# An MoE kernel's expert loop: ten tiles to a round, two of them half tiles, with each next tile's x transposed in the middle of a tile

## What is computed

```python
xn = _layernorm(x, axis=-1)                                  # x: (8, 2048, 256)
x = x + _L0_attn_ref(xn, W_qkv) + _L0_ffn_ref(xn, gate_w, ...)
# attention: one head of 256, causal, scores / 16
# ffn, on 16384 rows: shared swiglu 256 -> 512 -> 256, and
topk_ids = jnp.argmax(logits, axis=-1)                       # E = 32
xs = x * jax.nn.sigmoid(topk_val)[:, None]
sorted_x = xs[jnp.argsort(topk_ids)]
g = _grouped_mm(sorted_x, routed_gate_w, tokens_per_expert)
u = _grouped_mm(sorted_x, routed_up_w, tokens_per_expert)
d = _grouped_mm(jax.nn.silu(g) * u, routed_down_w, tokens_per_expert)
```

## Time and profile before

| | |
|---|---|
| median of 3 runs | 2384.75 us |
| profiled execution | 2384.18 us, its span 2382.2 us |
| mean granted TensorE clock | 0.992 |
| busy share of the span | PE 97%, PEld 90%, DVE 66%, ACT 51%, POOL 45% |
| token stage, expert stage, attention stage | about 0 to 703 us, 715 to 1445, 1451 to 2382 |
| instructions | 48635 |

### The profile page before, as it was taken

One profiled execution on the slowest core, in us unless ns is written; L12 is line 12 of the kernel. 1 busy time (PEld: TensorE's weight loads), 2 busy tenths in 40 slices (PEclk: granted clock), 3 DMA queues, 4 the chain that ended last, 5 costly groups with the idle time before them and its releaser, 6 DMA issues. The chain is left out here.

```text
span 2382.2 us, 48635 instructions
## 1 busy us (share of the span) xinstructions
PE 2316.4 (97%) x16118; PEld 2136.5 (90%) x16118; DVE 1565.0 (66%) x3322; ACT 1216.2 (51%) x2254; POOL 1065.6 (45%) x1031
## 2 busy tenths in 40 slices
PE   7999999999978999999999997999999999999998
PEld 6888888888868999999999995898988888888888
DVE  6777777777757777777777774646455555555555
ACT  3344434444425556656655653555555555555545
POOL 2333332333323333333333330666666666666667
PEclk9999999999998999999999999999999999999999
DMA  6665566665556766776767776334343444434331
GB/s 221 217 213 200 205 219 226 213 209 204 203 190 218 239 231 235 243 235 229 243 233 230 243 239 233 103 100 134 117 138 119 132 127 128 139 120 161 123 114 51
DMA packets 301977, 439.23 MB, mean 184 GB/s; under 512 B 35968, under 2 KB 209792, under 8 KB 301824
## 3 DMA queue, kind: packets, MB, share of 16 engines
q1 hardware_dynamic: 283712, 398.90, 48.9%
q0 software_dynamic: 18112, 38.37, 6.0%
HBM read 288.21 MB, written 148.96 MB: 184 GB/s over the span
## 5 line engine op out<-in xcount | busy, mean ns | idle before, releaser
L1231 POOL TENSOR_TENSOR t_p_lo<-t_score,t_p_hi 128x512 fp32r<-128x512 f32 (+1 forms) x320 | 360.0, 1131 | 190.7 <-ACT t_score L1355 113.9
L884 POOL DMA_INDIRECT ahead_rows<-xs_rows,ahead_slot x160 | 182.7, 1142 | 417.8 <-DMA ahead_slot<-token_of 257.7
L1347 ACT COPY t_score<-t_psS 128x512 f32<-128x512 f32 (+1 forms) x320 | 167.5, 523 | 332.5 <-PE t_psS L71 229.7
L1428 PE MATMUL t_psO<-t_v_hi,t_p_hi 128*128 128x258 f32 x1088 | 318.3, 293 | 0.9 <-DVE t_outb L1309 0.9
L1430 PE MATMUL t_psO<-t_v_hi,t_p_lo 128*128 128x258 f32 x1088 | 307.6, 283 | 0.0
L1432 PE MATMUL t_psO<-t_v_lo,t_p_hi 128*128 128x256 f32 x1088 | 306.6, 282 | 0.0
L1285 DVE TENSOR_TENSOR t_top<-t_top,t_psS 128x512 f32<-128x512 f32 (+3 forms) x264 | 155.1, 587 | 167.6 <-ACT t_score L1347 163.0
L305 POOL DMA_INDIRECT token_of<-a_token_i,a_slot_i x128 | 141.6, 1107 | 242.9 <-DVE a_slot_i L415 213.7
L69 PE MATMUL t_psS<-t_q_hi,ahead_x_hi 128*128 128x512 f32 (+3 forms) x640 | 233.8, 365 | 6.5 <-DVE t_q_lo L1267 5.5
L71 PE MATMUL t_psS<-t_q_lo,ahead_x_hi 128*128 128x512 f32 (+3 forms) x640 | 233.6, 365 | 0.0
L70 PE MATMUL t_psS<-t_q_hi,ahead_x_lo 128*128 128x512 f32 (+3 forms) x640 | 232.9, 364 | 0.0
(11 more groups left out here) (187 smaller groups left out, 7334.9 us busy)
## 6 DMA issues: line engine op xcount, KB each, us to landing
ahead_raw<-in_L_ffn_routed_gate_w SPq DMA_DIRECT2D x42, 512.0 KB
ahead_raw<-in_L_ffn_routed_up_w SPq DMA_DIRECT2D x42, 512.0 KB
ahead_raw<-in_L_ffn_routed_down_w SPq DMA_DIRECT2D x41, 512.0 KB, 5.0
e_raw<-in_L_ffn_routed_gate_w SPq DMA_DIRECT2D x41, 512.0 KB
e_raw<-in_L_ffn_routed_up_w SPq DMA_DIRECT2D x41, 512.0 KB
e_raw<-in_L_ffn_routed_down_w SPq DMA_DIRECT2D x41, 512.0 KB, 4.8
routed_rows<-e_dout SPq DMA_DIRECT2D x80, 256.0 KB, 4.4
a_xt<-in_L_attn_x SPq DMA_DIRECT2D x32, 512.0 KB, 5.9
```

The lines of the kernel that those rows point to most:

```text
L884: g.indirect_dma_start(out=xg[:, k, h], out_offset=None, in_=xs, in_offset=bass.IndirectOffsetOnAxis(slot[:, k, h:h + 1], 0)).then_inc(x_i ...
L1231: g_.tensor_tensor(p_lo[:, t % LR, c0:], score[:, t % SR, c0:], p_hi[:, t % HR, c0:].bitcast(F32), ALU.subtract).then_inc(lo_ok, 1)
L1347: s.copy(score[:, t % SR, c0:], psS[:, n % BANKS, c0:]).then_inc(u_act, 1)
L1428: nc.tensor.matmul(psO[:, a, 0:W], p_hi[:, kp, cols], v_hi[:, kv, j % J], start=j == 0, stop=False, skip_group_check=True)
```

## The change

- The expert loop runs in rounds of SETS = 10 tiles, of which places 4 and 9 hold half tiles of 128 rows; the first round is written out, the others are a loop of up to nine. An expert with c rows gets (c + 127) // 256 whole tiles, and a half tile where 1 to 128 rows are left. Whole tiles go to the eight whole places; half tiles to the half places, and to whole places if they don't fit.
- In a half tile x is stationary and the weights move, 512 columns at a time; h comes out with rows in partitions and is transposed (`h_transposes`) before `down_half`, which is done in the next step.
- `transposes(t + 1)` moves between the two halves q of `up(t)`, in a half tile between its gate and its up product; `x_high` and `x_low` move ahead with it.
- An expert's output rows lie together. Each tile's first row comes from a new table, `tile_row`, which SP reads before each store. The places behind are filled with zeros in 34 blocks of 128 rows instead of 32 of 256.
- `places()` makes constants on VectorE in the fifth group of the token stage; `tile_tables` is longer (30 operations instead of 16), and one more table row is copied.
- `keep.position` is made in the first round of the expert stage, two VectorE operations in each whole tile, and one at the end. In the attention stage its making goes; POOL waits there for the last stores before it gathers.

```diff
+SETS = 10
+HALVES = (4, 9)
...
+def is_half(j):
+    return j % SETS in HALVES
+
+
+def turns(j, i):
+
+    return SETS // 2 * i + j // 2
+
+
+def rows_moved(j, i):
+
+    k = j % 2
+    each = sum(1 if is_half(n) else 2 for n in range(k, SETS, 2))
+    return each * (i + j // SETS) + sum(1 if is_half(n) else 2 for n in range(k, j % SETS + 1, 2))
...
+            def places():
+
+                one, two = place_of[:, 0:1], place_of[:, 1:2]
+                then(v.tensor_scalar(by_ten[:], expert_f[:], float(SETS), None, ALU.mult))
+                then(v.tensor_scalar(tens[:], by_ten[:], float(SETS), token0[:, 0:1], ALU.add, ALU.is_le))
+                then(v.tensor_reduce(one, tens[:], AX.X, ALU.add))
...
             def tile_tables():
                 dve.wait_ge(seen_ok, J * NG + 1)
                 count = seen[:, NG % 2, 0]
-                then(v.tensor_scalar(tiles_i[:], count, float(ST - 1), None, ALU.add))
...
-                then(v.tensor_scalar(shift[:], shift[:], float(ST), None, ALU.mult))
+                full, whole = tiles_cum[:, 0, E - 1:E], tiles_cum[:, 1, E - 1:E]
+                index = wanted[:, 1:2]
+                flat = [a[:].rearrange("p a e -> p (a e)") for a in (tiles_cum, zeros, tiles, before_it, past, chosen, first_of)]
+                f_cum, f_zeros, f_tiles, f_before, f_past, f_chosen, f_first = flat
+                f_own, f_row = (a.rearrange("p a e -> p (a e)") for a in (own, row_of))
+                then(v.tensor_scalar(count_i[:], count, float(ST // 2 - 1), None, ALU.add))
...
+                v.tensor_scalar(tiles_i[:, 0], count_i[:], ST.bit_length() - 1, None, ALU.arith_shift_right)
+                then(v.tensor_scalar(tiles_i[:, 1], count_i[:], ST.bit_length() - 2, 1, ALU.arith_shift_right, ALU.bitwise_and))
...
+                then(v.tensor_scalar(more[:], by_eight[:, 0:SETS], full, None, ALU.is_lt))
...
+                then(v.tensor_reduce(rounds[:], more[:], AX.X, ALU.add))
...
+                if i == 4:
+                    places()
...
-            R = eng.value_load(keep.last_pair[0:1, 0:1], min_val=1, max_val=ET // 2 - 1)
-            for i in range(2):
-                for k in range(2):
-                    body(2 * i + k, k, i)
-            with eng.Fori(2, ET // 2) as i:
+            R = eng.value_load(keep.last_round[0:1, 0:1], min_val=1, max_val=ET // SETS - 1)
+            for j in range(SETS):
+                body(j, j, 0)
+            with eng.Fori(1, ET // SETS) as i:
                 with eng.If(i < R + 1):
-                    for k in range(2):
-                        body(2 * i + k, k, i)
+                    for j in range(SETS):
+                        body(SETS * i + j, j, i)
             return R
...
-            def load_slots(t, k, i):
-                wait_apart(sp, x_in[k], 16 * H * i, passed)
-                first = sp.value_load(keep.tile_slots[0:1, bass.ds(t, 1)], min_val=0, max_val=NS - 1)
-                sp.dma_start(slot[:, k], token_t[first]).then_inc(slot_in[k], 16)
-
-            def store(t, k):
-                wait(sp, do_ok, t + 1)
-                sp.dma_start(d_t[t], dout[:, k]).then_inc(d_out[k], 16)
+            def load_slots(t, j, i):
+                k = j % 2
+                wait_apart(sp, x_in[k], 16 * rows_moved(j - 2, i), passed)
+                unit = sp.value_load(keep.tile_slots[0:1, bass.ds(t, 1)], min_val=0, max_val=NS - 1)
+                if is_half(j):
+                    sp.dma_start(slot[:, k, 0:1], token_h[unit]).then_inc(slot_in[k], 16)
+                else:
+                    sp.dma_start(slot[:, k], token_t[unit]).then_inc(slot_in[k], 16)
+
+            def store(t, j):
+                k = j % 2
+                wait_apart(sp, do_ok, t + 1, passed)
+                row = sp.value_load(keep.tile_row[0:1, bass.ds(t, 1)], min_val=0, max_val=d_rows.shape[0] - ST)
+                if is_half(j):
+                    sp.dma_start(d_rows[bass.ds(row, P)], dout[:, k, 0]).then_inc(d_out[k], 16)
+                else:
+                    sp.dma_start(d_rows[bass.ds(row, ST)].rearrange("(p h) d -> p h d", h=H), dout[:, k]).then_inc(d_out[k], 16)
...
-            def step(t, k, i):
-                load_slots(t + 2, k, i + 1)
+            def step(t, j, i):
+                k = j % 2
+                load_slots(t + 2, j + 2, i)
                 load_up(t + 3, 1 - k)
                 load_down(t + 2, k)
                 if not is_first(t):
-                    store(t - 1, 1 - k)
+                    store(t - 1, j + SETS - 1)
...
+            def mul_half(t):
+                wait(dve, u_mm, Q * (t + 1))
+                wait(dve, silu_ok, Q * (t + 1))
+                wait(dve, hlo_ok, Q * t)
+                v.tensor_tensor(h32[:, 0], silu[:, 0], psU[:, 0].rearrange("p a n -> p (a n)"), ALU.mult).then_inc(h_ok, Q)
+
+            def h_low_half(t, k):
+                wait(dve, hhi_ok, Q * (t + 1))
+                v.tensor_tensor(h_lo[k][:, 0], psH[:], h_hi[k][:, 0].bitcast(F32), ALU.subtract).then_inc(hlo_ok, Q)
...
+            def positions(m):
+                ts = slice(m * TP, (m + 1) * TP)
+                wait(dve, pos_step, 2 * m)
+                v.tensor_tensor(moved[:], keep.one_hot[:, ts], keep.shift[:].unsqueeze(1).to_broadcast([P, TP, E]),
+                                ALU.mult).then_inc(pos_step, 1)
+                wait(dve, pos_step, 2 * m + 1)
+                v.tensor_reduce(begin[:, ts], moved[:], AX.X, ALU.add).then_inc(pos_step, 1)
...
+            def step(t, j, i):
+                k = j % 2
                 low(t + 1, 1 - k, 0)
-                mul(t, 0)
-                low(t + 1, 1 - k, 1)
-                h_low(t, k, 0)
-                mul(t, 1)
-                low_down(t, k)
-                x_low(t + 1, 1 - k)
-                h_low(t, k, 1)
-            tiles(dve, step)
+                if is_half(j + SETS - 1) and not is_first(t):
+                    h_low_half(t - 1, 1 - k)
+                if is_half(j):
+                    x_low(t + 1, j + 1)
+                    mul_half(t)
+                    low(t + 1, 1 - k, 1)
+                    low_down(t, k)
+                else:
+                    mul(t, 0)
+                    x_low(t + 1, j + 1)
+                    low(t + 1, 1 - k, 1)
+                    h_low(t, k, 0)
+                    mul(t, 1)
+                    low_down(t, k)
+                    if is_first(i):
+                        positions(sum(not is_half(n) for n in range(j)))
+                    h_low(t, k, 1)
...
+            def h_high_half(t, j, i):
+                wait(act, ht_mm, len(HALVES) * (i + j // SETS) + HALVES.index(j % SETS) + 1)
+                s.copy(h_hi[j % 2][:, 0], psH[:]).then_inc(hhi_ok, Q)
...
+                if is_half(j + SETS - 1) and not is_first(t):
+                    h_high_half(t - 1, j + SETS - 1, i - 1)
+                if is_half(j):
+                    silu_half(t)
+                    x_high(t + 1, j + 1)
+                    high(t + 1, j + 1, i, 1)
+                else:
+                    silu_of(t, 0)
+                    x_high(t + 1, j + 1)
+                    high(t + 1, j + 1, i, 1)
+                    h_high(t, k, 0)
+                    silu_of(t, 1)
+                    h_high(t, k, 1)
...
+            def up_half(t, j, i):
+                k = j % 2
+                wait(pe, xl_ok, t + 1)
+                for n, (psum, freed, out) in enumerate(((psG, silu_ok, g_mm), (psU, h_ok, u_mm))):
+                    wait(pe, wlo_ok, 2 * t + n + 1)
+                    wait(pe, freed, Q * t)
+                    for c in range(C):
+                        mm = split_matmuls(nc, psum[:, 0].rearrange("p a n -> p (a n)"), x_hi[:, k, c, 0:P], x_lo[:, k, c, 0:P],
+                                           part(whi, k, n)[:, c], part(wlo, k, n)[:, c], c == 0, c == C - 1)
+                    mm.then_inc(out, Q)
+                    if n == 0:
+                        transposes(t + 1, j + 1, i)
+
+            def h_transposes(t):
+                wait(pe, h_ok, Q * (t + 1))
+                for it in range(IT):
+                    mm = nc.tensor.transpose(psH[:, it * P:(it + 1) * P], h32[:, 0, it * P:(it + 1) * P], keep.ident[:])
+                mm.then_inc(ht_mm, 1)
...
+            def up(t, j, i):
+                k = j % 2
                 wait(pe, xl_ok, t + 1)
                 for q in range(Q):
+                    if q == 1:
+                        transposes(t + 1, j + 1, i)
...
-                up(t, k)
-                transposes(t + 1, 1 - k, i + k)
+            def step(t, j, i):
+                k = j % 2
+                if is_half(j):
+                    up_half(t, j, i)
+                else:
+                    up(t, j, i)
                 if not is_first(t):
-                    down(t - 1, 1 - k)
+                    if is_half(j + SETS - 1):
+                        down_half(t - 1, 1 - k)
+                    else:
+                        down(t - 1, 1 - k)
```

(31 more changed lines are left out.)

295 lines of the change are left out of this document (173 added, 122 removed).

## The result

The changed kernel takes **2552.08 us** (median of 4 runs, 2545.69 to 2555.02); the kernel before, beside it, 2385.36 (4 runs, 2382.60 to 2387.49). The ratio is 1.0696, 95% interval 1.0672 to 1.072: slower by 167 us. The forecast was 2424, with 2478 as its upper end. The direction was right; the size was missed by a factor of four.

What follows compares the result with a forecast made beforehand. TensorE, busy 97% of the span, was taken as the bound. Eight rounds at L = 13.4, half tiles' saving included, gave +34 us, clock +8, the rest -2: +40 on 2384.18, that is 2424 us; range 2345 to 2478.

Steps and rivals of the forecast that it cites:

- Half tiles, 64 us: Expert stage: a half tile takes TensorE 4.89 us instead of 8.87, 3.98 saved, times 16.
- Who waits for whom: Expert stage: TensorE's transposes of x wait for gathered rows, 80 to 110 us in all, longest near half tiles.
- the transposes of x wait for the gather in most tiles: Sign that the forecast is right: 80 to 110 us of such idle, whole steps of 9.5 to 10 us.
- 5 L + 26.0: Time in us of a round of ten tiles as five links; L is step start to x landed; at least 80.7.
- L = 13.4: Step start to x(t+2) landed after the change: 13.1 us, +0.7 table read, -0.4 loop turn; gives +34 us.
- Bounds 12.0 to 14.5: Lower and upper limits in us given for L, step start to x landed, around 13.1.
- Part *D: Rival: weight loads bind, half tiles needing 1.5 MB in 4.89 us; +10 us at most, counted in the range, no separate chance.
- Rival C: Weight and slot loads on SP slide with late x and share the gather's queue: L = 14.5, 2480 us; chance 0.15.
- Row table +0.7: In x's chain, the store on SP first reads its row number from a table: +0.70 us per link.
- Loop turn -0.4: In x's chain on SP, the loop's turn, 0.98 us, comes once in ten tiles instead of two: -0.4 on average.
- Clock +8: Expert stage: TensorE's clock falls after some waits, costing 8 us, between 0 and 25.
- The rest, -2: Tables +3, constants +1, skipped passes -3, positions -2, last half tile -1: sum -2 us, between -6 and +5.

Runs made afterwards that it cites:

- run 3: The changed kernel with slot numbers loaded one tile earlier, into five buffers in place of two: 2331.4 us, ratio 0.9787 to the kernel before.
- run 2: The kernel before with only the next x's transposes and split moved mid-tile, whole tiles only: 2551.65 us, ratio 1.0709.
- run 7: The whole-tile kernel with the mid-tile move, weight loads behind the first few cut to an eighth of their bytes: 2387.38 us, ratio 1.0009.
- run 8: The whole-tile kernel with the mid-tile move, down weights' load issued behind the next step's slot load: 2477.35 us, ratio 1.0396.
- run 1: The changed kernel with the next x's transposes and split back behind the second up half, half tiles kept: 2390.75 us, ratio 1.0031.
- run 6: The changed kernel with the store's row worked out from the round's number instead of read from the table: 2539.83 us, ratio 1.0644.
- run 5: The changed kernel with its eight rounds of ten tiles written out instead of a loop: 2538.49 us, ratio 1.0653.
- Run 12: The changed kernel with early slot numbers, and one gather in five held until its step has ended: 2441.63 us, ratio 1.0241.

## Why the prediction was wrong in size

**Half tiles, 64 us: right.** 62 in run 3. TensorE's steps were as worked out (a half step without a wait 6.06, with `down` of a whole tile in it).

**Who waits for whom: right.** Rows, in the two places near half tiles, and almost nothing on weights or VectorE. (Late before the change were three cases, not four: the wait of the earlier trace rows is one of the three of the earlier trace rows. No term of the sum hangs on it.) But only two waits per five tiles, not in most of them, and longer: "the transposes of x wait for the gather in most tiles" failed. In the steps between, 8.89 each, x was in time. The sum went by five equal links a round, 5 L + 26.0; in truth five tiles hang on one link that ends in the half step, one that starts behind it, and a plain step. With L = 13.4 for all of them that is 46.4 us instead of the 46.5 forecast, so this cost nothing; what cost was L.

**L = 13.4: the step that failed.** I took one L from the earlier trace rows, from a kernel in which x was in time and every tile whole, and kept it for every link. Bounds 12.0 to 14.5 held for one binding link only: the medians in the changed kernel are 14.5 where the half step asks, and 16.8 behind the half step; in run 2, without any half tile, the mean is 15.5. The two links' excess over 13.4, 1.1 and 3.4 us, is 4.5 us per five tiles, 72 us in all. The runs show three things that lengthen a link.

*The move.* `x_low` now stands ahead of the low part of the weights on VectorE, and SP's loads of the next weights, released by those, go out later: measured from the next step's start, the up weights at -1.3 us instead of -2.6 and the down weights at +0.5 instead of -0.2 (means of run 7, where x is almost never late, against the kernel before). The prediction had this slide at 1.3 us, and priced it at nothing, by the weights' two tiles of lead. The lead does cover the weights; it does not cover what stands behind them: store, slot load and gather queue with 0.5 to 1.5 MB. Run 8 takes away the order and gets 3.1 back (15.5 to 12.4), run 7 takes away the bytes and gets 5 (to 10.5).

*Lateness.* In run 2 the chain takes 15.9 us in the 54 steps in which TensorE waited, and 13.9 in the 15 in which it didn't. With the order of run 8 it is the other way round, 11.4 in the 34 with a wait and 13.5 in the 35 without. So lateness as such doesn't set the price; the order of the loads beside it does.

*The half step.* The link that starts behind it takes 16.3 us already in run 1, with the transposes late. So most of its excess is not the move's. The turn of the loop is part of it: 18.1 us with a turn, 16.0 without (17.9 and 15.5 in run 1). For the rest the trace shows only this: in run 1 the down weights go out 0.6 us behind the step start there, right ahead of the store, and before the step start in all other steps. That they are the cause is not shown; no run takes the half step's weights away by themselves. Part *D* had priced these loads at 10 us at most, again by their lead.

Rival C had the mechanism of the move, gave it 0.15 and L = 14.5, and its 2480 was still 72 us too low.

**Row table +0.7: right as a duration** (0.6 in run 6), but no link got shorter by it. **Loop turn -0.4: wrong in sign where it counts.** It comes once in ten, but one turn of the long loop costs SP 4 to 5.5 us instead of 1, in a chain that binds: about +14 (run 5). It takes the read of the row table to make it so long: in run 6 the turn costs 1.1. The two terms were priced apart, and their cost is in their meeting.

**Clock +8: wrong, about +64.** The stage is 895.4 - 670.8 = 224.6 us longer than in run 3, which does the same work; 164.2 - 4.0 = 160 are waits, and the other 64.4, 1.9 for each of 34 waits, are matmuls at the lower clock. The traces' clock records say the same: over the time in which TensorE was busy in the stage, what the granted clock fell short of full speed sums to 68.5 us in the change and 4.4 in run 3. Run 12 gives 2.0 a pause when nothing else is late. I had one row of a pause of 2.21 us and took 1 us a round; each round held four waits. Run 2 has 170.3 - 126.1 = 44 us in 60 waits of 2.1 us, 0.7 each. Set against the waiting, the clock adds 0.40 in the change, 0.35 in run 2, 0.38 in run 12.

**The rest, -2: +7 before the stage and +1.5 behind it.** Tables took 3 us more, as said, and TensorE waits 2.6 us for them in two places; TensorE's pause behind the loop's end went from 4.3 to 2.6, less than the 3 us promised, and the one at the entrance of the attention stage from 7.1 to 11.5, though that one lies between 6.5 and 12.6 in the other runs whatever their edit.

Together, on the stage: 64 predicted off, 62 came off; waits against a full TensorE 98 forecast, 160 came; clock 8 forecast, 64 came. 118 of the 128 us missed are in these two, and both grow from the one wrong assumption, that every link of the new kernel is as long as those of the old one.

What stays open: which of the two, the shared DMA engines or the order within SP's own queue, delays the 1 KB slot load, was not separated; runs 7 and 8 fit both. Why SP needs 4 to 5.5 us at the long loop's turn stays open too; runs 5 and 6 show that it goes away with the loop, and all but 1.1 us of it with the read of the row table.

## What to carry to other kernels

When a change asks for data sooner, look for the smallest load in the chain that brings it, and issue that one earlier, before anything is asked sooner: here 1 KB of slot numbers, one tile earlier, turned +167 us into -52. Don't price a chain by its length in the kernel before: ask which loads the change releases later, and what then waits behind them, and read it for each kind of step apart. In this kernel, pauses of TensorE of 2 to 5 us cost a third to 0.4 of their length on top, for the clock.

## What the runs showed of the hardware

A load of 1 KB took 1.7 us to land with light traffic, 2.3 ahead of a 0.5 MB load, and 3.9 behind one (runs 7, 8, 2); a gather of 128 KB 2.9, 3.8 and 5.5. Mean traffic says little: run 3 moved 250 GB/s with one wait on rows, run 2 190 with 60 of them.

A turn of a loop whose body is ten steps long cost SP about 4 to 5.5 us between a store and the next slot load, one of two steps about 1. Written out straight, the two followed each other by 1.2 us nearly everywhere (run 5). With one table read less in each step of the same loop of ten, a turn cost 1.1 us (run 6).

The granted clock stood at 0.50 (1.2 GHz) a few microseconds behind a pause of 3.75 us and back at 1.00 (2.4 GHz) 2.5 us further on; pauses of 5 us cost 1.9 to 2.0 us beyond themselves, pauses of 2 us 0.7.
